# Two attention steps at once in a fused transformer kernel, with its fills, derived weights and MLP start in a new order

## What is computed

```python
def block_0(x, c, context):
    shift_a, scale_a, gate_a, shift_m, scale_m, gate_m = split(silu(c) @ W_mod + b_mod, 6)
    qkv = (ln(x) * (1 + scale_a) + shift_a) @ W_qkv + b_qkv
    x = x + gate_a * (attention(qkv) @ W_proj + b_proj)          # 16 heads, softmax
    x = x + attention(ln(x) @ W_qc + b_qc, ln(context) @ W_kvc + b_kvc) @ W_cproj + b_cproj
    h = gelu((ln(x) * (1 + scale_m) + shift_m) @ W_mlp1 + b_mlp1) @ W_mlp2 + b_mlp2
    return x + gate_m * h

def block_1(x, anchor, bank):
    nx = ln(x) * gamma + beta
    evidence = softmax(nx @ Wq @ (bank @ Wk).T * H ** -0.5) @ (bank @ Wv)
    combined = concat(nx, evidence, anchor)
    probs = softmax(combined @ router_W + router_b)
    routed = sum_e(probs_e * (silu(combined @ e_w1_e + e_b1_e) @ e_w2_e + e_b2_e))
    g = sigmoid(silu(combined @ gate_w1 + gate_b1) @ gate_w2 + gate_b2)
    return x + g * (routed @ out_w + out_b)
```

## Time and profile before

| | |
|---|---|
| time, median of 3 runs (least, most) | 641.93 us (640.37, 642.57) |
| the profiled execution, time / span of its instructions | 643.52 / 641.6 us |
| PE, DVE, ACT, POOL busy | 586.7, 455.6, 387.5, 204.4 us |
| mean granted TensorE clock | 0.960 |
| start, to the first shifted scores | 42.17 us |
| attention rounds 0 to 7 | 42.17 to 373.13 us |

### The profile page before, as it was taken

One profiled execution on the slowest core, in us unless ns is written; L12 is line 12 of the kernel. 1 busy time (PEld: TensorE's weight loads), 2 busy tenths in 40 slices (PEclk: granted clock), 3 DMA queues, 4 the chain that ended last, 5 costly groups with the idle time before them and its releaser, 6 DMA issues.

```text
span 641.6 us, 16396 instructions
## 1 busy us (share of the span) xinstructions
PE 586.7 (91%) x6153; PEld 378.5 (59%) x6153; DVE 455.6 (71%) x1267; ACT 387.5 (60%) x893; POOL 204.4 (32%) x230
## 2 busy tenths in 40 slices
PE   3679999999999998998999979998999999999996
PEld 3354555555555554554566534444687897797785
DVE  7487888889898898999883334554556855865654
ACT  2237677777777766776774464455547646655762
POOL 6637435244352335434502111112332232123000
PEclk9769999999999999999998599999999999999998
DMA  7524553343323441333300001000001001000000
GB/s 198 123 78 115 164 135 104 99 119 96 95 61 89 113 121 54 88 104 101 98 11 4 2 0 34 1 1 1 16 18 34 18 18 33 16 16 17 16 17 18
DMA packets 48555, 39.24 MB, mean 61 GB/s; under 512 B 6209, under 2 KB 47842, under 8 KB 48482
## 3 DMA queue, kind: packets, MB, share of 16 engines
q1 hardware_dynamic: 46296, 34.49, 20.1%
q10 hardware_dynamic: 2186, 3.77, 2.0%
HBM read 9.93 MB, written 2.10 MB: 19 GB/s over the span
## 4 chain that ended last, share of the span: by engine, by line
PE 65%; DVE 16%; ACT 8%; issue 5%; SPq 3%; DMA 3%; ACTq 0%; POOL 0%; DVEq 0%; POOLq 0%
PE PS L896 28%; PE PS L1698 9%; PE PS L1669 7%; PE PS L1749 5%; DVE NM L1504 3%; PE PS L1682 3%; PE PS L933 2%; PE PS L1761 2%; SPq L1266 2%; PE PS L1742 2%; PE PS L1720 2%; DMA Qs<-MT 2%; DVE XN L1590 2%; PE PS L1754 2%; PE PS L1728 1%
## 5 line engine op out<-in xcount | busy, mean ns | idle before, releaser
L1385 ACT ACTIVATE PR<-PS 128x512 f32<-128x512 f32 x256 | 151.6, 599 | 47.0 <-PE PS L1682 42.6
L1504 DVE TENSOR_REDUCE NM<-PS 128x4 f32<-128x512 f32 x256 | 165.9, 680 | 15.9 <-PE PS L1669 15.8
L1698 PE MATMUL PS<-PR,Va 128*32 128x128 f32 x2048 | 111.8, 292 | 0.0
L1682 PE MATMUL PS<-Qs,Ks 64*128 64x128 bf16 x1024 | 104.0, 224 | 2.6 <-ACT PR L1385 1.5
L1669 PE MATMUL PS<-Ks,Qs 64*128 64x128 bf16 x1024 | 102.4, 223 | 3.9 <-DMA Qs<-Qp 2.0
L1669 PEld LDWEIGHTS PS<-Ks,Qs 64*128 64x128 bf16 x1024 | 58.6, 96 | 77.4 <-issue 45.9
L707 ACT ACTIVATE r_HID<-PS,ANC 128x128 f32<-128x128 f32 x224 | 63.3, 371 | 41.8 <-PE PS L896 41.8
L1682 PEld LDWEIGHTS PS<-Qs,Ks 64*128 64x128 bf16 x1024 | 58.7, 96 | 9.6 <-issue 4.9
L896 PE MATMUL PS<-r_NXS,r_WNS 128*128 128x512 f32 x168 | 54.1, 430 | 5.4 <-ACT r_HID L707 5.4
L1698 PEld LDWEIGHTS PS<-PR,Va 128*32 128x32 f32 x2048 | 40.9, 109 | 27.9 <-issue 2.5
L896 PE MATMUL PS<-r_EVS,r_US 128*128 128x512 f32 x168 | 47.6, 392 | 0.0
(11 more groups left out here) (184 smaller groups left out, 1065.7 us busy)
## 6 DMA issues: line engine op xcount, KB each, us to landing
Qs<-Qp SPq DMA_DIRECT2D x96, 128.0 KB
Ks<-Kp SPq DMA_DIRECT2D x90, 128.0 KB
CTXG<-in_ctx SPq DMA_DIRECT2D x8, 256.0 KB, 4.0
r_CTX<-in_ctx SPq DMA_DIRECT2D x8, 256.0 KB, 2.7
out<-X SPq DMA_DIRECT2D x8, 256.0 KB, 2.3
X<-in_x SPq DMA_DIRECT2D x7, 256.0 KB, 6.4
W<-in_weights ACTq DMA_DIRECT2D x2, 855.0 KB
Qs<-MT SPq DMA_DIRECT2D x62, 8.0 KB
```

Source lines behind the costliest of these rows:

```text
L1385: nc.scalar.activation(PR[:, u, :], T_BANK[u % 2][:, :], ACT.Exp, scale=SCALE)\
L1504: nc.vector.tensor_reduce(out=NM[:, c.b // 2, c.second, u // 2, u % 2 * 4:u % 2 * 4 + 4], in_=S_BANK[score_bank(c, u)[0]][:, :].rearrange( ...
L1682: last = nc.tensor.matmul(T_BANK[u % 2][:, j * P:(j + 1) * P], Ks[c.stack][rows, lo + j, cols], Qs[c.stack][rows, lo + j, cols], start=Tru ...
L1698: last = nc.tensor.matmul(O_BANK[p.turn][TW * j:TW * j + TW, at:at + P], Va[c.mem][:, c.b, 4 * (u // 2) + j, u % 2 * TW // 2:u % 2 * TW // ...
```

## The change

1. Steps are emitted in pairs: score t+14, shifted t, score t+15, shifted t+1, then the values of t-2 and t-1. The turns move by up to a step; `max_turn` and `o_turn` come between the shifted and the value part.
2. The times of all fills and their reads are set anew, so that nearly each double step holds one. K and Q moves to the second stack are apart (21 and 26). The statistics of `ln_x` for groups 4 and 6 come one round earlier (`early_statistics`).
3. `ln_x` is normalised by GpSimd (two operations of 512 columns) instead of VectorE (four of 128). The read of `proj_s` of group 7 goes from VectorE to ScalarE.
4. `DERIVED` is in another order, and VectorE reads `wo_high`, in two instructions.
5. Group 1's MLP steps are woven into round 8, and `between_cores` does step 2 only.

```diff
-OF_SECOND_STACK = (1, 3)
+OF_DVE = ()
+READ_BY_ACT = (1, 3, 7)
...
 def norm_steps(t, name, g):
-    if name == "ln_x":
+    if name == "ln_x" and g in OF_DVE:
...
-            + fill_steps(3.9, "q0", i + 1, (0, 4.0), (1, 4.4))
-            + fill_steps(5.9, "k0", i + 1, (0, 6.0), (1, 6.4))
+            + fill_steps(4.0, "q0", i + 1, (0, 4.1), (1, 4.2))
+            + fill_steps(7.0, "k0", i + 1, (0, 7.1), (1, 8.0))
...
+def early_statistics(i):
+
+    return stats_steps(26.2, 28.2, "ln_x", 2 * i - 4) + norm_steps(29.0, "ln_x", 2 * i - 4)
...
-DERIVED = ("keys", "u_low", "u_high", "wo_low", "wo_high", "bias_out", "anchor")
+DERIVED = ("keys", "bias_out", "anchor", "u_low", "u_high", "wo_low", "wo_high")
...
-            + [(20 + 0.5 * k, 1, i + 1, *m) for k, m in enumerate(moves("K") + moves("Q"))])
+    return (steps + [(17.0, 1, i + 1, "zero", 0)] + [(21 + 0.5 * k, 1, i + 1, *m) for k, m in enumerate(moves("K"))]
+            + [(26 + 0.5 * k, 1, i + 1, *m) for k, m in enumerate(moves("Q"))])
...
-        for w in range(8):
+        for w in range(0, 8, 2):
             t = 8 * p + w
-            if (i, t) == (NG, 8):
-                yield ("between",)
             yield from stack_moves(t, t + 1)
             if w == 2 and ahead1:
                 yield ("max_parts", ahead1)
-            if w == 5 and back1:
+            yield from group_steps(t, t + 1)
+            if (i, t) == (NG, 8):
+                yield ("between",)
+            for at in (t, t + 1):
+                yield from step("score", at + LEAD)
+                yield from step("shifted", at)
+            yield from stack_moves(t + 1, t + 2)
+            if w == 2 and ahead1:
+                yield ("max_turn", ahead1, ahead1.n - bool(here))
+            if w == 4 and back1:
                 yield ("o_turn", back1, back1.n + 1 + bool(here) + bool(ahead1))
                 yield ("o_norm", back1)
-            yield from group_steps(t, t + 0.5)
-            c, u = core(LEAD)
-            if c:
-                yield ("score", c, u)
-            for name, ahead in (("shifted", 0), ("value", -2)):
-                c, u = core(ahead)
-                if c:
-                    yield (name, c, u)
-            if w == 7 and back1:
+            yield from group_steps(t + 1, t + 2)
+            for at in (t, t + 1):
+                yield from step("value", at - 2)
+            if w == 6 and back1:
                 yield ("o_back", back1)
-            if w == 3 and ahead1:
-                yield ("max_turn", ahead1, ahead1.n - bool(here))
-            yield from group_steps(t + 0.5, t + 1)
...
-    for i in range(1, 3):
-        for step in valid_steps(MLP_STEPS, i):
-            body(*step)
+    for step in valid_steps(MLP_STEPS, 2):
+        body(*step)
...
+            elif name == "wo_high":
+                dve.wait_ge(bank_filled["derive"], DERIVED.index(name) + 1)
+                hidden = GROUP_BANK[:, 2 * P:2 * P + NHC * B].rearrange("p (c b) -> p c b", b=B)
+                at = V_COLS["be1"][0]
+                nc.vector.tensor_tensor(ANC[:, :, :], hidden, V[:, at:at + NHC].unsqueeze(2).to_broadcast([P, NHC, B]),
+                                        ALU.add)
+                nc.vector.tensor_copy(WO[:, GT:EH * P], GROUP_BANK[:, 0:EH * P - GT])\
+                    .then_inc(bank_read["derive"], 1)
```

More of the change, by code:

```diff
@@ new lines, in regular_steps @@
+            + fill_steps(7.0, "k0", i + 1, (0, 7.1), (1, 8.0))
+            + fill_steps(10.0, "v1", i, (1, 10.1))
+            + fill_steps(12.0, "proj_c", i - 3, (1, 12.1))
+            + fill_steps(14.0, "yt_c", i - 3, (1, 14.1))
+            + fill_steps(16.0, "xt_c", i - 1, (1, 16.1))
+            + fill_steps(18.0, "k1", i + 1, (0, 18.1), (1, 19.0))
+            + fill_steps(21.0, "xt_x", i - 1, (1, 21.1))
+            + fill_steps(23.0, "q1", i + 1, (0, 23.1), (1, 24.0))
+            + fill_steps(26.0, "v0", i + 1, (1, 26.1))
@@ L284, in stack_steps @@
         return steps + [(23 + 0.1 * k, 1, 0, *m) for k, m in enumerate(moves("Q"))]
[L285 to L288 removed]
+    crossed = HOLDS[0][i + 1][0] == CROSS
+    steps, first, second = [(1.0, 0, i + 1, "zero", 0)] if i > 0 else [], *("KQ" if crossed else "QK")
+    steps += [(8 + 0.5 * k, 0, i + 1, *m) for k, m in enumerate(moves(first))]
+    steps += [(11 + 0.5 * k, 0, i + 1, *m) for k, m in enumerate(moves(second))]
+    return (steps + [(17.0, 1, i + 1, "zero", 0)] + [(21 + 0.5 * k, 1, i + 1, *m) for k, m in enumerate(moves("K"))]
+            + [(26 + 0.5 * k, 1, i + 1, *m) for k, m in enumerate(moves("Q"))])
 def stack_of(mem, it):
@@ L433, in later, with mlp_and_router @@
     return not isinstance(g, int) or g > 0
-def mlp_and_router(nc, stack, X, ctxin, w, vec, rows1, condT, mod, gbm, half, zeros, YT, ident, PS, load_w2, out,
+def mlp_and_router(nc, stack, X, V, ctxin, w, vec, rows1, condT, mod, gbm, half, zeros, YT, ident, PS, load_w2, out,
                    bank_filled, bank_read, max_done, exp_done, o_normed, o_stored):
@@ L651, in split_weights @@
             elif k > 1:
-                pool.wait_ge(bank_read["derive"], k)
+                pool.wait_ge(bank_read["derive"], DERIVED.index(("u_low", "u_high")[k - 2]) + 1)
             to, source = (WNS, w("e_nx", lo, hi - lo)) if k < 2 else (US, U[:, lo:hi])
@@ L1148, in build_block @@
         sync_programs, gpsimd_programs, scalar_programs, vector_programs, tensor_programs = mlp_and_router(
-            nc, stack, X, ctxin, w, vec, rows1, condT, mod, gbm, half, zeros, YT, ident, PS, load_w2, out,
+            nc, stack, X, V, ctxin, w, vec, rows1, condT, mod, gbm, half, zeros, YT, ident, PS, load_w2, out,
             bank_filled, bank_read, max_done, exp_done, o_normed, o_stored)
@@ L1319, in body @@
                     nc.gpsimd.memset(Ks[2][:, :, :].bitcast(F32), 0.0).then_inc(stack_init, 1)
-                elif name == "norm" and ev[1] != "ln_x" and not (ev[1] == "ln_s" and at_first(ev[2])):
+                elif name == "norm" and not (ev[1] == "ln_x" and ev[2] in OF_DVE) and not (ev[1] == "ln_s" and at_first(ev[2])):
                     g, k = ev[2], LN_KIND[ev[1]]
@@ L1455, in body @@
                     extra["mlp"]("xt_read", 0, 0, 0, 0)
-                elif ev[:2] == ("read", "proj_s") and ev[2] in OF_SECOND_STACK:
+                elif ev[:2] == ("read", "proj_s") and ev[2] in READ_BY_ACT:
                     _, name, g, part = ev
@@ L1583, in body @@
                     last.then_inc(bank_read[name], 1)
-                elif ev[:2] == ("norm", "ln_x"):
+                elif ev[:2] == ("norm", "ln_x") and ev[2] in OF_DVE:
                     g, k, b = ev[2], LN_KIND[ev[1]], ev[3]
@@ L1593, in body @@
                         last.then_inc(ln_done[k], 1)
-                elif ev[:2] == ("read", "proj_s") and ev[2] not in OF_SECOND_STACK:
+                elif ev[:2] == ("read", "proj_s") and ev[2] not in READ_BY_ACT:
                     _, name, g, part = ev
```

107 lines of the change are left out of this document (48 added, 59 removed).

## The result

The changed kernel takes 618.77 us (median of 4 runs, 617.23 to 619.34), the kernel before 641.66 in the same comparison: a ratio of 0.961, 95% interval 0.956 to 0.966. That is 22.9 us less. The prediction of 604 was 15 us too low; 618.8 lies inside its range of 596 to 622. The profiled executions stand at 618.3 and 643.5, with spans of 616.6 and 641.6, so what follows splits up 25 us of span.

A forecast was written before the change was run, and what follows sets the result against it. TensorE sets the rounds (95% busy), VectorE close behind at 90%. Rounds 1 to 6 20.9, round 0 2.5, round 7 12.8, close 2.5: 38.7 less gives 604.8 or 603.2, said as 604 us; range 596 to 622.

The forecast's parts named there:

- favourite: Whole kernel: the attention, round 7 and close gain as reckoned, 598 to 609 us; chance 50%.
- B: Round 7: attention gains, but the clock falls again for 14 to 24 us, giving back 6 to 10: 612; chance 25%.
- C: Rounds: bursts on VectorE and ScalarE, or casts waiting for GpSimd, take half the saving back, 38.5 a round: 616; 15%.
- flat 36.7 a round: Rounds 1 to 6: VectorE's 33.2 us over a 0.905 busy share; six rounds take 220.2, 20.9 less.
- step 2, max_parts, and step 18: Places in a round expected late; step 2 has ln_x statistics and max_parts with no fill to cover them.
- 0.2 a round: Casts of the maxima: mean grows some 0.05 us with GpSimd busier, 0.2 a round, counted within the 36.7.
- The bound: Rounds 1 to 6: VectorE's 33.2 us at its sustained 90% busy share decides, not TensorE's 34.3.
- The double step: Attention loop: 1.13 us against 1.38 for two plain steps, 16 times a round, 4.0 us less TensorE work.
- Round 0: First round, starting at the lower clock, otherwise like the others: 2.5 us less (bounds 0 and 4.0).
- Round 7: Last round: clock holds (9.6), double steps save 4.0, 0.8 given back for ScalarE: 12.8 us less, 37.5.
- The close: After the last values: MLP steps of group 1 fill TensorE's waits of 0.91, 0.78 and 1.41: 2.5 us less.
- the 1.5 that the prediction named as a sign of being right: Close: the waits should be under 1.5 us together.

The follow-up runs named there:

- e2: Changed kernel with the fills of rounds 5 and 6 at their regular-round places, reads over a double step ahead of the cast: 608.5 us, ratio 0.944.
- e10: Kernel before with only ln_x's normalisation moved to GpSimd: ratio 1.002, rounds 1 to 4 157.33 us in place of 158.10.
- e6: Changed kernel with ln_x normalised by VectorE as before, not GpSimd: 623.22 us.
- e5: Kernel before with only the loop in double steps (close's first fill moved behind the last turn): rounds 1 to 4 161.93 us against 158.10.
- e4: Changed kernel with the single-step loop of before, everything else at its new place: rounds 1 to 4 150.26 us.
- e12: Changed kernel, regular places in rounds 5 and 6, GpSimd's q0, q1, k0 splits behind the maxima's parts, context normalisation at step 6: ratio 0.943.
- e7: Changed kernel with the old order of the derived weights (u_low, u_high, wo_low, wo_high ahead of bias_out and anchor): ratio 0.957.
- e9: Changed kernel, regular places in rounds 5 and 6, GpSimd's q0, q1, k0 splits behind the maxima's parts, context normalisation behind the split: 612.09 us, ratio 0.945.
- e8: Changed kernel with group 1's MLP steps behind the close again, as before: ratio 0.961.
- e11: Changed kernel with the old order of derived weights and wo_high read by ScalarE in eight instructions: round 7 44.9 us in place of 39.2.
- e3: Changed kernel, GpSimd's splits of q0 and q1 in rounds 5 and 6 waiting for the maxima's parts: four waits ahead of max_turn gave 3.3 us.

## Why the prediction was right, and where its sum was off

The change gains, and the time lies in the range. But it lies outside the favourite's own 598 to 609: the parts came to 25.0 us less (of span) where 38.7 were added up. The range holds the time because it took in B and most of C.

- **Rounds 5 and 6.** The step that failed is the flat 36.7 a round: "the six rounds then take 220.2, 20.9 less". They took 228.9, 12.2 less, 8.7 us off. Rounds 1 to 4 were 3.2 better than reckoned (143.6 against 146.8), rounds 5 and 6 11.9 worse (85.3 against 73.4). Of the latter e2 took back 10.0 by places alone: 13.6 us of low clock at 0.42 make 5.7 (an estimate), which leaves 4.3, and the waits ahead of max_turn fell by 3.1 (2.08, 1.38, 2.08 and 1.38 to 1.11, 0.37, 1.11 and 1.28). The prediction had named the place ("step 2, max_parts, and step 18") and the price of an overlapped cast (0.89 each), but spread it as 0.2 a round over all rounds, and had nothing for the subtraction, which stretches too (0.97 and 1.04). In the crossed rounds the order itself set the read and its split against the cast, every time. That could have been read from the order: VectorE's row of q0 stands next to the cast there, and not in a regular round. The 0.2 itself was too small: the casts' mean in rounds 1 to 4 grew from 0.281 to 0.453 us, 0.7 a round. The new places did that and not GpSimd's new work, for the move alone (e10) gives 0.311.
- **The bound.** VectorE reached 93.6% and not 90.5%, on 33.6 us of work and not 33.2: 35.9 in place of 36.7. e6 shows the same share with more work, so more work for VectorE costs its full length, as said. That it is the only bound isn't shown, with TensorE at 97.1%.
- **The double step.** 4.0 us of TensorE's work a round was the right size at the old places (3.8, e5) and too much at the new ones (2.5 between e4 and the changed kernel, where the places had taken 1.0 already); TensorE's own 34.3 came out as 34.85. What the prediction didn't credit are the new places: without them the double step loses (rival C's mechanism, at its full size of 5.9 us of waiting a round). It took the place changes as neutral, and they were the condition.
- **Round 0**: 0.6 in place of 2.5. The double steps take 3.0 off TensorE's 37.09, but it stands 1.39 for an exponential, 1.07 for a reduce and 1.35 ahead of max_turn, where k0's split overlaps the subtraction. In e12 that last wait is 0.63.
- **Round 7**: 12.6 against 12.8, in part by luck. At 0.4 a us (the price below) the 23.9 low ones cost 9.6, so 3.0 are left for the double steps less ScalarE's share; 9.6 and 3.2 were predicted. But the reason given, that wo_high's new place keeps the clock up, isn't borne out by the timed runs of e7, and in e4 and e9 the clock fell in this round with the new order.
- **The close**: 2.1 against 2.5 (e8: 2.8 to 3.5). Of the waits that the weaving should fill only a part went: TensorE stands 3.0 us in the stretch of the changed kernel where it stood 4.1, twice the 1.5 that the prediction named as a sign of being right. The longest is still that for ScalarE's read of m_XT, 1.75 where it was 1.41:

```profile
356.38 1.10 PE L1775 MATMUL PS<-OgT,W 128*128 128x512 f32 x2 [0.94 <-ACT OgT L1424]
366.10 0.63 PE L947 MATMUL PS<-ident,m_XN 128*128 128x128 f32 x4 [1.75 <-ACT m_XT L705]
```

- **Behind the close**: 0 predicted, 2.5 lost to low clock from 425.99 to 432.82. The wait of 1.45 us that stands there (427.00, TensorE for VectorE's r_NX) is in both kernels; before, the clock held.
- **Rivals.** B said the clock would fall again, in round 7. It fell in rounds 5 and 6, at waits that the change made, and behind the close: its sign, "a stretch of low clock past 300 us", came, at 426 and not in round 7. Its 612 was nearer than the favourite's 604, but for another place. C was nearest, with 616: it had "casts wait for GpSimd" and rounds of 38.5, and the six rounds took 38.1 in the mean, all of the excess in two of them.

Open is what decides a fall. The same waits of 2.08 and 1.38 us, twice each, were followed by three low stretches in the changed kernel and e7, and by one in e6, e8 and e11; in e4, e7 and e9 low stretches began with TensorE busy without a gap. The Trainium skill, TensorE: Matmul & The Clock Gate, Part 1, names the low clock the idle state; these stretches don't fit that as the only cause. Nor does the sum of the waits order the falls: in rounds 5 and 6 those ahead of max_turn make 3.9 us in e2, without a fall, and 3.7 in e3, with one in each round. That e2's places keep the clock up in more than one execution is shown by its timed runs; why they do is not.

## What to carry to other kernels

When a loop is made coarser, the work it saves appears only if every hand-over around it still has a whole coarse step of room; look in the order for the places where a short operation on the critical path stands next to a long one, or next to one that releases work on an engine that shares a port with it, and count those at full price, not as an average. Test the parts apart: here the coarser loop alone lost 1.0 us a round, the move to GpSimd alone gave nothing, the new places with the move gave 2.0, and all together 3.6. Before an operation is pushed back behind a wait, follow the buffer that it frees to the transfer that waits for it, and see what stands behind that transfer in its queue.
